# A four-layer network of attention and routed experts on one core: kept gated experts, another order of attention tiles, a moved bias table

## What is computed

```
x = x + L0_ffn(L0_cond(x, bias[16,1024,1024], mask, ...))  # attention, given bias; MoE: 16 experts, 1 choice, 128 tokens each
x = x + L1_ffn(L1_cond(x, ...))          # gated MoE: 8 experts, 2 choices, a shared expert; MoE: 8 experts, 2 choices, gelu
x = x + L2_ffn(L2_cond(x, ...))          # attention, bias from positions; product-key experts and a gated MLP
x = x + L3_ffn(L3_cond(x, ...))          # gated MoE as in L1; MoE: 8 experts, 1 choice, silu

# attention: 16 heads of 64, one key and value head for all, one extra (null) key
sim = q @ concat(null_k, k).T + concat(null_bias, bias)   # causal and padding mask, softmax, @ concat(null_v, v)
# L2's bias: a small MLP over the 2047 distances (only those up to the diagonal count)
h = silu(ln(pos @ w0 + b0, g0)); h = silu(ln(h @ w1 + b1, g1)); h = h @ w2 + b2; bias = h[i - j]
# gated expert: (leaky(x @ w_gate) * (x @ w_up)) @ w_down, 128 hidden units: 384 KB of weights per expert
# MoE of L0 and L3: act(x @ W1 + b1) @ W2 + b2, 1024 hidden units: 2 MB per expert; of L1: 512 hidden, 1 MB per expert
```

## Time and profile before

| | us |
|---|---|
| median of 3 runs | 3312.52 (3308.84 to 3315.05) |
| the profiled execution's own time | 3311.75 |
| its span in the trace | 3309.5 |
| TensorE busy | 2595.6 (78%) |
| VectorE (DVE) busy | 1648.9 (50%) |
| ScalarE (ACT) busy | 1378.0 (42%) |
| GpSimd (POOL) busy | 779.8 (24%) |
| mean granted clock of TensorE | 0.906 of full speed |

### The profile page before, as it was taken

One profiled execution on the slowest core, in us unless ns is written; L12 is line 12 of the kernel. 1 busy time (PEld: TensorE's weight loads), 2 busy tenths in 40 slices (PEclk: granted clock), 3 DMA queues, 4 the chain that ended last, 5 costly groups with the idle time before them and its releaser, 6 DMA issues. The chain is left out here.

```text
span 3309.5 us, 59545 instructions
## 1 busy us (share of the span) xinstructions
PE 2595.6 (78%) x16144; PEld 2013.3 (61%) x16161; DVE 1648.9 (50%) x4672; ACT 1378.0 (42%) x3221; POOL 779.8 (24%) x1015
## 2 busy tenths in 40 slices
PE   5799999984977533892669999998599997653595
PEld 2467777774966532561346777777577777542585
DVE  3477766643124135222766776664588884315111
ACT  2366666741322221330346666774244441222121
POOL 0032333212023043004123223231233322105001
PEclk9999999996988875996889999999899998895798
DMA  8521212102853574112002122210200001462785
GB/s 300 200 86 59 83 61 86 57 15 81 321 129 115 178 262 162 48 57 81 1 29 84 60 80 64 85 58 15 73 1 0 0 0 36 141 182 84 261 313 179
DMA packets 173776, 341.72 MB, mean 103 GB/s; under 512 B 21830, under 2 KB 125254, under 8 KB 167344
## 3 DMA queue, kind: packets, MB, share of 16 engines
q1 hardware_dynamic: 161328, 307.99, 27.8%
q0 software_dynamic: 12288, 31.83, 3.4%
HBM read 266.71 MB, written 83.17 MB: 106 GB/s over the span
## 5 line engine op out<-in xcount | busy, mean ns | idle before, releaser
L750 DVE CUSTOM_DVE_ANT_0 prob_l<-ps_s,bias_l,nsn 128x1024 f32<-128x1024 f32 (+3 forms) x256 | 277.1, 1083 | 183.9 <-DVEq L749 182.0
L683 PE MATMUL ps_s<-khi,stage 128*128 128x512 f32 (+5 forms) x768 | 342.1, 445 | 10.2 <-POOL stage L657 10.1
L814 ACT ACTIVATE prob_l<-prob_l,nmax 128x1024 f32<-128x1024 f32 (+3 forms) x256 | 252.2, 985 | 66.1 <-DVE nmax L750 63.1
L683 PE MATMUL ps_s<-klo,stage 128*128 128x512 f32 (+5 forms) x768 | 264.1, 344 | 0.0
L950 POOL DMA_INDIRECT yg<-slot_outputs,slot x128 | 131.0, 1023 | 460.1 <-PEq L88 422.2
L677 PE MATMUL ps_s<-km,ident 128*128 128x384 bf16 (+6 forms) x688 | 210.7, 306 | 0.4 <-DVE nmax L750 0.2
L648 POOL COPY nsn<-nsn 128x4 f32 (+1 forms) x128 | 24.1, 188 | 783.3 <-DVE diff L767 650.0
L716 PE MATMUL ps_o<-pT_l,v 128*64 128x256 f32 x1664 | 207.8, 387 | 0.0
L657 POOL TENSOR_TENSOR stage<-qo,stage 64x256 fp32r<-64x256 f32 x256 | 188.4, 736 | 46.9 <-POOLq L656 46.9
L806 ACT ACTIVATE pT_l<-ps_pt 128x512 f32<-128x512 f32 x256 | 152.8, 597 | 99.2 <-PE ps_pt L691 95.9
L1506 ACT ACTIVATE hT<-ps_h,ws 128x128 f32<-128x128 f32 x312 | 89.1, 369 | 238.1 <-PE ps_h L1479 238.1
(11 more groups left out here) (326 smaller groups left out, 5983.6 us busy)
## 6 DMA issues: line engine op xcount, KB each, us to landing
ws<-in_L_ffn_experts_dram SPq DMA_DIRECT2D x39, 2052.0 KB, 7.5
ws<-in_L_cond_experts_dram SPq DMA_DIRECT2D x78, 384.0 KB, 3.4
xs<-slot_rows SPq DMA_DIRECT2D x156, 128.0 KB, 2.0
slot_outputs<-ys SPq DMA_DIRECT2D x156, 128.0 KB, 2.3
slot_rows<-zero_sb SPq DMA_DIRECT2D x1, 17280.0 KB, 53.7
slot_outputs<-zero_sb SPq DMA_DIRECT2D x1, 17280.0 KB, 103.8
bias_l<-in_fside_16xSxS_dram SPq DMA_DIRECT2D x16, 512.0 KB, 3.8
mlp_w<-in_L_ffn_experts_dram SPq DMA_DIRECT2D x8, 1024.0 KB, 18.4
```

The source lines that it names most:

```text
L683: ins = pe.matmul(ps_s[:, u, at:at + hi - lo], stage[:, x.s, x.h % 2, x.h // 2, :], att[part][:, b * S + lo:b * S + hi], start=False, stop ...
L750: dve.tensor_tensor_reduce(out=spans(x, prob), in0=scored(x), in1=spans(x, bias), scale=-1.0, scalar=nsn[:, s, h:h + 1], op0=ALU.add, op1= ...
L814: act.activation(prob[x.s][:, x.h, 0:x.W], prob[x.s][:, x.h, 0:x.W], ACT.Exp, bias=nmax[:, x.s, x.h:x.h + 1], scale=-1.0, accum_out=rsum[: ...
```

## The change

1. `core_phase`: a half's 8 slots alternate between the long and the short tile, head by head. Short scores have one bank of their own, `ps_h`; long scores have the two double banks, `ps_l`. Outputs, totals and null terms are done once per half for both tiles. The lags are new. TensorE's instructions are the same ones in another order.
2. `glu_experts_phase`: the 8 gated experts (3 MB) are loaded in the route before (`Experts`) and kept on chip. GpSimd reads the expert's number and copies its 128x768 into the tile's buffer, eight tiles deep; SP only loads rows and stores outputs. The first eight tiles have a fixed place: tile t is the first of expert t (`rows_of`, `expert_of`).
3. Outputs are stored in the order of tiles (`t * P`). `finish` computes each token's place in that order as well as its row for the scatter; `slot_outputs` is no longer cleared.
4. `FirstWeights`: in layers 0 and 3 the weights and `b2` of the first four tiles are loaded by SP during the route ahead.
5. In the gated MoEs' routes rows are turned 10 tiles ahead (was 6) through 16 buffers (was 8); the shared expert's weights have their own semaphore.
6. `BiasTable` moves out of the route of layer 1's second MoE into the combination at the end of layer 1, where DVE adds gathered rows between its steps.

The core of the diff:

```diff
                 self.W = (self.qt + 1) * P
-                self.quad = (p * G + g) * 4 + w // 4
-                self.n = self.quad * 4 + self.h
-
-                self.pair = p * G + g
-                self.long = (self.pair * 2 + self.b) * 4 + self.h
+                self.group = p * G + g
+                self.pair = self.group * 2 + self.b
+                self.n = self.pair * 4 + self.h
+                self.begins = w % 8 == 0
...
-            units(pe, (0, scores), (9, first_values), (11, second_values), (12, turned_back), (4, transposes))
...
+            units(pe, (0, scores), (12, all_values), (3, turn_short), (5, turn_long), (14, turned_back))
...
-            units(dve, (13, outputs), (0, negated), (1, null_differences), (4, second_blocks), (3, totals))
...
+            units(dve, (15, outputs), (0, negated), (5, second_blocks), (7, null_differences), (10, totals))
...
-            units(act, (11, outputs), (4, first_blocks), (0, exponentials), (2, null_probability))
...
+            units(act, (13, outputs), (3, short_blocks), (5, long_blocks), (1, exponentials), (8, null_probability))
...
-    AHEAD = 6 if shared is not None else 0
-    RING = 8 if shared is not None else 2
+    AHEAD = 10 if shared is not None else 0
+    RING = NT if shared is not None else 2
...
 def rows_of(eng, r, t):
 
+    if isinstance(t, int) and t < 8:
+        return t * T
     return eng.value_load(r["tile_row"][0:1, bass.ds(t, 1)], min_val=0, max_val=SLOT_ROWS - P)
...
+def expert_of(eng, r, t):
+
+    if isinstance(t, int) and t < 8:
+        return t
+    return eng.value_load(r["tile_expert"][0:1, bass.ds(t, 1)], min_val=0, max_val=7)
...
+class FirstWeights:
...
+    def __init__(self, nc, ctx, name, w, b2):
+        self.w, self.b2, self.sem = w, b2, nc.alloc_semaphore(f"{name}_first_weights")
+        self.ws = ctx.enter_context(nc.sbuf_tensor(f"{name}_ws", [P, 4, w.shape[2]], F32))
+        self.b2s = ctx.enter_context(nc.sbuf_tensor(f"{name}_b2s", [P, 4, D], F32))
+
+    def load(self, sp):
+        for e in range(4):
+            sp.dma_start(self.ws[:, e], self.w[e]).then_inc(self.sem, 16)
+            sp.dma_start(self.b2s[:, e, :], row(self.b2, D, e * D)).then_inc(self.sem, 16)
...
                 first = rows_of(sp, r, t) if by_map else t * P
                 sp.dma_start(xs[:, u, :], xs_dram[bass.ds(first, P), :]).then_inc(loads[u], 16)
+                if isinstance(t, int) and t < 4:
+                    sp.wait_ge(first_weights.sem, 8 * 16)
+                    sp.sem_inc(loads[u], 32)
+                    return
                 sp.dma_start(ws[:, u], w[bass.ds(e, 1)].rearrange("a p f -> p (a f)")).then_inc(loads[u], 16)
                 sp.dma_start(b2s[:, u, :], b2[bass.ds(e, 1), :].to_broadcast([P, D])).then_inc(loads[u], 16)
 
             def store(t, u):
-                first = rows_of(sp, r, t) if by_map else t * P
                 sp.wait_ge(dve_y.sem, dve_y.after("y", t))
-                sp.dma_start(ys_dram[bass.ds(first, P), :], ys[:, u, :]).then_inc(stores[u], 16)
+                sp.dma_start(ys_dram[bass.ds(t * P, P), :], ys[:, u, :]).then_inc(stores[u], 16)
...
-                sp.dma_start(ys_dram[bass.ds(first, P), :], ys[:, u, :]).then_inc(stores[u], 16)
+                sp.dma_start(ys_dram[bass.ds(t * P, P), :], ys[:, u, :]).then_inc(stores[u], 16)
...
+        @block.gpsimd
+        def _(gp):
+            gp_w.open(gp)
+            gp.wait_ge(experts.sem, experts.count)
+
+            def weights(t, u):
+
+                e = experts.of(gp, r, t)
+                gp.wait_ge(pe_y.sem, pe_y.after("y", t - BUF))
+                gp.wait_ge(gp_w.sem, gp_w.after("weights", t - 1))
+                gp.sem_inc(gp_w.sem, 1)
+                gp.tensor_copy(ws[:, u], at(experts.w, e)).then_inc(gp_w.sem, 1)
+
+            pipeline(gp, n_tiles, BUF, (0, weights))
...
             def hidden(t, u):
                 pe.wait_ge(act_x.sem, act_x.after("xT", t))
+                pe.wait_ge(gp_w.sem, gp_w.after("weights", t))
...
 
         @block.vector
         def _(dve):
             dve_g.open(dve)
-            for t in range(NT):
-                gather.add(dve, t, yg, dve_g)
+            todo = list(range(NT))
+
+            def rows_added(n):
+                for t in todo[:n]:
+                    gather.add(dve, t, yg, dve_g)
+                del todo[:n]
+
+            if table:
+                table.vector(dve, rows_added)
+            rows_added(NT)
...
+    def vector(self, dve, between):
         NTP = S // P
...
             ins.then_inc(self.moments, 1)
+            between(2)
...
-                      clear=(xs_dram, ys_dram, slots_cleared))
+                      clear=(xs_dram, slots_cleared))
```

More of the change, by code:

```diff
@@ L555, in core_phase @@
-        act_t = ph.steps("first", 8)
-        dve_t = ph.steps("second", 8)
+        gp_s = [ph.steps("null hi0 waited0 lo0 hi1 waited1 lo1") for _ in range(2)]
+        pe_s = [ph.steps("scores", 8) for _ in range(2)]
+        dve_s = [ph.steps("waited neg", 8) for _ in range(2)]
+        act_s = [ph.steps("exp", 8) for _ in range(2)]
+        pe_t = [ph.steps("turned", 8) for _ in range(2)]
+        pe_u = ph.steps("turned", 8)
+        act_t = [ph.steps("out", 8) for _ in range(2)]
+        dve_t = ph.steps("out", 8)
@@ new lines, in scores, with turn, turn_short @@
+                ins.then_inc(pe_s[s].sem, 1)
+            def turn(x, bank, first, end):
+                for k in range(first, end):
+                    ins = pe.transpose(ps_pt[:, bank, (k - first) * P:(k - first + 1) * P], prob[x.s][:, x.h, k * P:(k + 1) * P],
+                                       c["ident"][:])
+                return ins
+            def turn_short(x):
+                if x.s:
+                    pe.wait_ge(act_s[1].sem, act_s[1].after("exp", x.n))
+                    pe.wait_ge(act_t[0].sem, act_t[0].after("out", x.n - 1))
+                    turn(x, 0, 0, x.qt + 1).then_inc(pe_t[1].sem, 1)
@@ L734, in _ @@
                 s.open(dve)
             def negated(x):
[L737 removed]
+                s, h, b = x.s, x.h, x.b
                 if h == 0:
[L739 to L746 removed]
```

469 lines of the change are left out of this document (244 added, 225 removed).

## The result

| | before | changed |
|---|---|---|
| median, us | 3312.43 (3308.84 to 3315.05, 4 runs) | 3157.55 (3152.37 to 3160.31, 4 runs) |
| profiled execution, us | 3311.75 | 3152.37 |
| span, us | 3309.5 | 3150.7 |

The ratio is 0.9531, with a 95% interval of 0.9514 to 0.9548: faster by 155 us. The forecast was 3182, faster by 130, and the measured time lies in the range (3108 to 3265). Sign and size of the sum were right; single terms were not: the gated stages and the cores gave 48 us more than forecast, and four routes put at 0 cost 20.

The account below looks back on a forecast made before the run. Cores bound by TensorE, gated stages by SP's reads and DMA issues, the route by a chain of waits. 3311.75 - 57 - 55 - 13 - 15 - 6 - 30 + 22 + 24 = 3182 us, range 3108 to 3265.

Parts of the forecast that it names:

- Gated experts: Gated-expert stages, layers 1 and 3: experts kept on chip, 1.8 us a tile, 87 us against 144 and 143; -57 and -55.
- Rule against row: GpSimd's 768-column copy: 0.78 us by the trace's copy row, 2.07 us by the skill's half-of-VectorE rule; the row was used.
- rival two: Gated stages: GpSimd's copy is the bound at 2.35 us a tile, +43, 3225 us; chance 0.15.
- Experts of layers 0 and 3: First four tiles' weights loaded during the route, so first transposes start earlier (-9, -10); -13 and -15 in all.
- The lead over the loads: Experts of layers 0 and 3, after the fifth tile: TensorE is ahead of the loads, some -2.5 and -2 us.
- The routes ahead of them: Routes before experts of layers 0 and 3: 0; 0 to +5 if slowed by the 8 MB ahead, 0 in layer 0.
- Cores: Attention cores: same TensorE instructions in another order, small waits; -3 a layer, -6, bounds -20 and +20 per layer.
- Route of layer 1's second MoE: Without the bias table the scatter follows the gathers directly, ending at about 1278 instead of 1308; -30 (-27 to -31.6).
- the table in the combination: End of layer 1: the table's 64 us chain plus 3.5 stands against 46 us now; +22 (+15 to +26).
- The null phase: Layer 2: the mask lands only with the spread, first use 33 or 34 us after the spread's issue, not 9.2; +24.
- The gated routes: Gated MoEs' routes, layers 1 and 3: extra DVE operations and the shared weights' own semaphore cancel to about 0.
- The rivals: Mask overtakes spread 3158us, 0.12; GpSimd bound 3225, 0.15; TensorE half clock 3283, 0.07; copies exposed 3453, 0.05; SP unlifted 3276, 0.04.

Follow-up runs that it names:

- e6: Changed kernel with GpSimd's copy of the expert's weights done twice per tile: 3177.70 us.
- e11: Changed kernel with the core's products with the values in three visits a half where it has one: 3170.12 us.
- e3: Changed kernel with the spread DMA issued behind the weight loads of layer 2's projection phase: 3125.19 us, ratio 0.9435.
- e4: Changed kernel with AHEAD back at 6 tiles (was 10), 16 buffers kept: 3141.40 us.

## Why the prediction was right, and where it was not

**Gated experts (-57, -55; measured -69.4, -69.0).** The mechanism held: SP's reads and issues were the bound, the copy is hidden (0.83 us where 0.78 was worked out), and the clock is up (0.94). Two sizes were off. TensorE's pace was taken from the neighbouring tiles of the earlier trace rows, 1.72 us; undisturbed it is 1.54. And SP's 1.65 us were in fact 1.81, which TensorE feels only from the 23rd tile on. The row of 1.72 us came from a stage in which TensorE lived on its loads, and was an upper end, not the work itself. Of the 12 us that layer 1's stage is under its 87, the tiles give 8 (put at 39 x 1.8 and 4 for a cold start, 74 in all; 1.69 a tile with the start included, 66), and the terms around them 4: the first transposes come after 2.5 us where 3.5 stood, pipeline and last store take 6 where 9 stood.

**Rule against row.** The copy's row was right. The Trainium skill ("Trainium Architecture — The Big Picture", section "The five engines, in one table") calls GpSimd half as fast as VectorE for streaming elementwise work. For this plain float32 copy the trace does not agree: 827 ns for 768 columns is 1.1 ns a column, where VectorE's 128x512 copy, out of PSUM, takes 689 ns, 1.3 a column. A VectorE copy between the same memories stands in no row. What twice the copy's price would have done e6 shows: 13 us a stage, where rival two had 21.

**Experts of layers 0 and 3 (-13, -15; -13.4, -16.4).** The first step held: the first transposes come 2.5 and 3.0 us into the phase, 9.5 and 9.6 us earlier than before. (The list of signs has "some 9 us after their phase begins"; the sum itself has about 3.) The steps behind it did not, and made up for each other. From the first tile's transposes to the fifth's it is 21.2 and 23.6 us, 6.8 and 5.6 less than before, where 1.5 and 2.8 less were put. The lead over the loads that was worth another 2.5 and 2 us is not there: layer 0's remaining tiles take 2.8 us more than before, with 5.4 us of waits for loads from the sixth tile on (826.23), layer 3's 1.0 less. As these phases vary by some 6 us from run to run, a hit within 2 us is luck.

**The routes ahead of them** were put at 0, with 0 to +5 named and dropped for layer 0 since "nothing large is moved" there. For layer 3's route no such look was taken: there 32 gathers share the DMA engines with 8 MB, and they landed after 7.8 us in place of 2.8. That is the step that failed: +5.6 there, +1.8 in layer 0.

**Cores (-3 each; -14.6, -13.4).** The largest error in kind. The prediction took "the same instructions in another order" as the same work, and looked only for waits, of which there were few; the waits in fact grew. What shrank was TensorE's busy time, with the number of visits to the products with the values: e11 prices one at 0.18 to 0.29 us, the trace of the kernel before at 0.29. "Cores within 5 us of 539" was the sign that should have shown, and did not.

**Route of layer 1's second MoE (-30; -32.4)** and **the table in the combination (+22; +18.1 with the kept experts, which took 2 us less).** Right: the scatter's 31.6 us wait is gone, and its 32 DMAs start 1.6 us after the last gather's issue (the 3 to 5 us put in for its landing are not waited for). What was late next is what was named, GpSimd's own queue:

```profile
L967 POOL DMA_INDIRECT yg<-slot_outputs,slot x32: 1002/1006/1218, 1100.3 to 1141.4; - x32
...
L1122 POOL DMA_INDIRECT slot_rows<-cur_sb,slot_out x32: 979/979/1031, 1143.0 to 1182.9; - x32
```

**The null phase (+24; +30.5).** Right in kind, shown by e3: the mask does land only with the spread. Two sizes were short. The turnover between the spread's issue and the mask's was put at 4 us and is 1.8, so that 2 us more of the wait fall into the null phase. And the first use comes 37.5 us after the spread's issue, not 33 or 34: the spread takes 36.3 to land, where it took 34.2, and the loads behind it another 1.2. The 14.90 us for which the mask's issue held SP (for want of room in the queue, it seems; e3 shows only that it goes with the spread) are a surprise, but seem to have cost nothing: all four loads are issued 11 us before the spread is in.

**The gated routes (0; +6.5, +6.3).** "Some seven more small operations" and a semaphore were weighed, and the change of AHEAD was not. The work that ends this route is the shared expert's, so the step to ask was what the four more tiles ahead push back. e4 returns 12 us with one number.

**The rivals.** None came true: the mask did not overtake the spread, GpSimd is no bound, the clock is high, the cores' copies stayed covered, and SP's limit did move (3.64 to 1.81 us). The errors stood on both sides (26 us on the gated stages, 22 on the cores; against that 20 on the routes and 6 on the null phase), so the sum came out closer than its terms, which is luck.

## What to carry to other kernels

Two orders of the same matmuls are not the same work: look at the times from one start to the next where TensorE goes from one kind to another, and have few of the visits that cost something (here those to the values, and hardly those for turning back). Before a large DMA is issued, look at what is queued behind it and needed at once; the same transfer a few instructions later cost 3 to 5 us in place of 30. And where work is brought forward on an engine, ask what ends the phase: if it is the work that is pushed back, nothing is won.

## What was not expected of the hardware

- A visit to the products with the values (weights of 128x64 between others of 128x128) cost TensorE 0.29 us by the times between starts, with no wait in the trace, and 0.18 to 0.29 by e11's cores; a visit for turning back (128x128) cost under 0.05.
- A DMA's issue on SP took 14.90 us while an 8 MB DMA of 2048 rows stood ahead of it in the queue, and 0.35 us without.
- 8 MB of loads beside indirect gathers took these from 2.8 to 7.8 us to land, while GpSimd's issue of one stayed at 1.0 us.
